# Experts' stage on the score banks, opened inside the last step of head 5

## What is computed

```python
xn = _layernorm(x)
qkv = einsum('bld,ed->ble', xn, w_qkv)      # 16 heads of 16, rope on q and k
attn = softmax(einsum('bhlm...', q, k) * scale)
s = einsum(attn, v) @ w_out.T
expert_idx = argmax(xn @ gate_w.T)          # 8 experts, one for each row
inter = square(relu(xn @ wg[e])) * (xn @ wu[e])
g = silu(inter @ wd[e])
return x + s * g
```

## Time and profile before

| | us |
|---|---|
| median of 3 runs (1563.64 to 1586.98) | 1569.34 |
| profiled execution | 1570.67 |
| its span | 1567.9 |
| TensorE busy (share of the span) | 1512.0 (96%) |
| DVE busy | 1383.9 (88%) |
| ACT busy | 1234.6 (79%) |
| mean share of full TensorE clock | 0.98 |

### The profile page before, as it was taken

One profiled execution on the slowest core, in us unless ns is written; L12 is line 12 of the kernel. 1 busy time (PEld: TensorE's weight loads), 2 busy tenths in 40 slices (PEclk: granted clock), 3 DMA queues, 4 the chain that ended last, 5 costly groups with the idle time before them and its releaser, 6 DMA issues.

```text
span 1567.9 us, 35612 instructions
## 1 busy us (share of the span) xinstructions
PE 1512.0 (96%) x13217; PEld 622.3 (40%) x13217; DVE 1383.9 (88%) x1497; ACT 1234.6 (79%) x2381; POOL 150.1 (10%) x206
## 2 busy tenths in 40 slices
PE   6997999999998999999999999999999999999997
PEld 4553333333374333333333333333333333333336
DVE  6678789999845999999999999999999999999706
ACT  4642388888756888888888888888888888888880
POOL 4432322100000222000010000000000000000100
PEclk9999599999999999999999999999999999999999
DMA  5873244326254445333333342233332433332203
GB/s 193 272 188 120 52 82 81 59 42 116 32 153 118 79 84 122 46 45 46 45 44 44 44 98 42 39 42 44 45 46 44 98 45 44 44 44 31 66 5 124
DMA packets 77909, 117.95 MB, mean 75 GB/s; under 512 B 29073, under 2 KB 64273, under 8 KB 70801
## 3 DMA queue, kind: packets, MB, share of 16 engines
q1 hardware_dynamic: 71808, 103.99, 33.9%
q0 software_dynamic: 3072, 8.39, 2.1%
q10 hardware_dynamic: 2896, 3.62, 0.6%
HBM read 75.31 MB, written 39.85 MB: 73 GB/s over the span
## 4 chain that ended last, share of the span: by engine, by line
PE 90%; ACT 3%; DVE 3%; DMA 2%; issue 2%; SPq 0%; ACTq 0%
PE ps L1139 42%; PE ps L1152 37%; PE ps L1071 3%; PE ps L1072 2%; DMA arena<-xs_d 1%; ACT arena L591 1%; ACT arena L555 1%; PE ps L1281 1%; DVE arena L699 1%; PE ps L1130 1%; PE ps L1095 1%; PE ps L1250 1%; PE ps L1238 1%; PE ps L1082 1%; DMA arena<-orec_d 1%
## 5 line engine op out<-in xcount | busy, mean ns | idle before, releaser
L591 ACT ACTIVATE arena<-ps 128x512 f32<-128x512 f32 x2048 | 1111.8, 595 | 179.0 <-PE ps L1139 91.1
L733 DVE TENSOR_REDUCE arena<-ps 128x1 f32<-128x1024 f32 x992 | 1205.5, 1221 | 38.8 <-PE ps L1130 32.9
L1139 PE MATMUL ps<-qs,ks 50*128 50x512 f32 x2048 | 759.0, 450 | 2.8 <-ACT arena L591 2.6
L1130 PE MATMUL ps<-ks,qs 48*128 48x512 f32 x1984 | 739.3, 453 | 4.5 <-DVE arena L733 2.9
L1152 PE MATMUL ps<-arena 128*32 128x256 f32 x8192 | 661.5, 395 | 7.4 <-ACT arena L555 7.0
L1139 PEld LDWEIGHTS ps<-qs,ks 50*128 50x128 f32 x2048 | 306.5, 187 | 434.1 <-issue 429.9
L1152 PEld LDWEIGHTS ps<-arena 128*32 128x32 f32 x8192 | 162.9, 108 | 386.2 <-issue 386.1
L1130 PEld LDWEIGHTS ps<-ks,qs 48*128 48x128 f32 x1984 | 298.6, 188 | 10.3 <-DVE arena L733 8.0
L1001 POOL COPY arena<-v_sb 128x256 f32 (+1 forms) x32 | 13.3, 416 | 953.2 <-ACT arena L555 938.1
L1071 PE MATMUL ps<-arena 128*128 128x512 f32 x128 | 67.8, 611 | 0.7 <-ACT arena L504 0.7
L513 ACT COPY arena<-ps 128x512 f32<-128x512 f32 x32 | 18.8, 586 | 54.8 <-PE ps L1072 54.8
(11 more groups left out here) (104 smaller groups left out, 510.4 us busy)
## 6 DMA issues: line engine op xcount, KB each, us to landing
qs<-parts_d SPq DMA_DIRECT2D x186, 128.0 KB, 4.5
ks<-parts_d SPq DMA_DIRECT2D x186, 128.0 KB, 5.1
parts_d<-arena SPq DMA_DIRECT2D x64, 256.0 KB, 2.6
xs_d<-arena SPq DMA_DIRECT2D x13, 384.0 KB, 3.5
arena<-xs_d SPq DMA_DIRECT2D x13, 384.0 KB, 3.9
ys_d<-arena SPq DMA_DIRECT2D x13, 384.0 KB, 2.8
onum_d<-arena SPq DMA_DIRECT2D x128, 32.0 KB
arena<-onum_d SPq DMA_DIRECT2D x3, 1024.0 KB
```

The costliest lines, as they stand in the source:

```text
L591: nc.scalar.activation(prob[kb % 2][:, c * W:(c + 1) * W], ps[:, bank, :], ACT.Exp, scale=SCALE).then_inc(exp_done[bank], 1)
L733: nc.vector.tensor_reduce(most[head_slot][:, tile, u:u + 1], ps[:, AB + 2 * u:AB + 2 + 2 * u, :], AX.XY, ALU.max).then_inc(a_reduced[u], 1)
L1130: ins = nc.tensor.matmul(ps[:, AB + c, :], qs[head_slot][ABASE:ABASE + KR, tile * P:(tile + 1) * P].bitcast(F32R), ks[head_slot][ABASE:ABA ...
L1139: nc.tensor.matmul(ps[:, bank, :], ks[s][0:KS, kb * P:(kb + 1) * P].bitcast(F32R), qs[s][0:KS, c * W:(c + 1) * W].bitcast(F32R), start=Tru ...
```

## The change

- The bank of a score comes from a table made for a pair. It counts 0, 1, 2 as before, but score 28 takes the second oldest bank instead of the oldest (`BENDS`), so that the last four scores of a pair have banks 2, 1, 0, 2.
- The experts' stage uses the score banks: transposes in bank 0, gate and up products in banks 1 and 2, and Y in banks 6 and 7 in turn (bank 7 alone before). A Y product waits for the Silu before the last one.
- `open_experts` issues, in the last step of head 5 between the two halves of the value product, the read of the first tile's expert and the first transposes. The step issues no scores of head 6. Three of them are issued in the stage's last iterations, the fourth behind the stage as before.
- The waits for the sums' copy and for DVE's last reduce move to the first transpose of hidden rows and the first Y.
- ACT takes a Silu of one element first, then copies the first turned tile, then the sums. The exponential of one column at the end is left out.
- SP asks for group `g + 3` where it asked for `g + 2`.
- `expert_of(i + 1)` stands at the end of iteration `i`; `expert_of(i)` stood before the product of tile `i`.

```diff
+    TB, EB, YB = 0, 1, 6
+        BENDS = (28,)
+        def banks_of_pair():
+            oldest_first, banks = list(range(NBB)), []
+            for n in range(2 * KB * QT):
+                banks.append(oldest_first.pop(1 if n in BENDS else 0))
+                oldest_first.append(banks[-1])
+            return banks
...
                 for g in range(NF // FG):
-                    if XR <= g + XR - 1 < NF // FG:
-                        load_sorted(g + XR - 1)
+                    if g + XR < NF // FG:
+                        load_sorted(g + XR)
                     store_sorted(g)
...
             def experts():
+                nc.scalar.activation(table_in[:, 1:2], table_in[:, 0:1], ACT.Silu)
+                turned_out(0)
                 sums_out(1, FB - 1)
-                turned_out(0)
...
-                act.wait_ge(xs_out, NF)
-                nc.scalar.activation(xsT[0][:, 0, 0:1], xsT[0][:, 0, 0:1], ACT.Exp)
...
-                        with_b = not (last_pair and s == 1 and kb == KB - 1)
+                        with_b = not (held_back or (last_pair and s == 1 and kb == KB - 1))
...
                             if c % 2:
                                 weigh_values(pi, s, kb, c // 2)
+                                if held_back and c == 1:
+                                    open_experts()
...
+            def open_experts():
+                for c in range(QT):
+                    pe.wait_ge(exp_done[b_bank(1, KB - 1, c)], past(b_before(FB - 1, 1, KB - 1, c) + 1))
+                pe.wait_ge(expert_ready, 1)
+                expert_of(0)
+                turn_sorted(0)
...
             def experts():
-                for u in range(2):
-                    pe.wait_ge(a_reduced[u], past(FB * 2 * KB + AHEAD - KB))
-                pe.wait_ge(o_out[1], past(FB))
-                turn_sorted(0)
...
+                    if i == NF:
+                        pe.wait_ge(loaded[0], (FB + 1) * (16 * LOADS))
+                        pe.wait_ge(shift_loaded[0], (FB + 1) * 64)
+                        pe.wait_ge(xs_out, NF)
+                        first_scores((0,))
                     if 1 <= i <= NF:
+                        if i == 1:
+                            pe.wait_ge(o_out[1], past(FB))
...
                     if i >= 2:
+                        if i == 2:
+                            pe.wait_ge(a_reduced[1], past(FB * 2 * KB + AHEAD - KB))
                         pe.wait_ge(inter_out, i - 1)
-                        if i >= 3:
-                            pe.wait_ge(y_out, i - 2)
-                        nc.tensor.matmul(ps[:, AB + 3, 0:D], interT[(i - 2) % 2], wd2[:, bass.ds(which.pop(i - 2), 1), :],
+                        if i >= 4:
+                            pe.wait_ge(y_out, i - 3)
+                        nc.tensor.matmul(ps[:, YB + i % 2, 0:D], interT[(i - 2) % 2], wd2[:, bass.ds(which.pop(i - 2), 1), :],
                                          start=True, stop=True).then_inc(y_done, 1)
-                pe.wait_ge(hu_ready, NF)
+                    if i + 1 < NF:
+                        expert_of(i + 1)
+                    if i == NF:
+                        pe.wait_ge(hu_ready, NF)
+                        first_scores((1, 2))
```

More of the change, by code:

```diff
@@ L279, in layer_kernel @@
         NP = NH // 2
-        BUSES = [[len(range((i - s) % NBB, KB * QT, NBB)) for i in range(NBB)] for s in range(2)]
-        PAIR_BUSES = [BUSES[0][i] + BUSES[1][i] for i in range(NBB)]
+        BENDS = (28,)
[5 more added lines that the diff above has]
+            return banks
+        BANKS = banks_of_pair()
+        PAIR_BUSES = [BANKS.count(i) for i in range(NBB)]
         NB2 = KB // 2
@@ L292, in past, with place_in_pair @@
             return n + 1
+        def place_in_pair(s, kb, c):
+            return (s * KB + kb) * QT + c
         def b_bank(s, kb, c):
-            return (kb * QT + c + s) % NBB
+            return BANKS[place_in_pair(s, kb, c)]
         def b_before(pi, s, kb, c):
-            bank = b_bank(s, kb, c)
-            return pi * PAIR_BUSES[bank] + (s * BUSES[0][bank] + (kb * QT + c) // NBB)
+            n = place_in_pair(s, kb, c)
+            return pi * PAIR_BUSES[BANKS[n]] + BANKS[:n].count(BANKS[n])
         block = ctx.enter_context(nc.Block())
@@ L574, in experts @@
                             act.wait_ge(inter_ready, i - 1)
-                        nc.scalar.activation(hr[i % 2], ps[:, AB + 1 + i % 2, 0:DE], ACT.Relu).then_inc(relu_done, 1)
+                        nc.scalar.activation(hr[i % 2], ps[:, EB + i % 2, 0:DE], ACT.Relu).then_inc(relu_done, 1)
                     if i >= 2:
@@ L580, in experts @@
                             act.wait_ge(y_stored[g % XR], g // XR * 16)
[L581 to L583 removed]
+                        nc.scalar.activation(ysb[g % XR][:, z, :], ps[:, YB + i % 2, 0:D], ACT.Silu).then_inc(y_out, 1)
             def exps(pi, s, first):
@@ L1191, in pair @@
                         for c in range(QT):
-                            if with_b and not (held_back and c == QT - 1):
+                            if with_b:
                                 score(b_pi, b_slot, (kb + 1) % KB, c)
@@ L1206, in turn_sorted, with expert_of, first_scores @@
                 for k in range(KC):
-                    last = nc.tensor.transpose(ps[:, AB, k * P:(k + 1) * P], xs[g % XR][:, z, k * P:(k + 1) * P], ident[:])
+                    last = nc.tensor.transpose(ps[:, TB, k * P:(k + 1) * P], xs[g % XR][:, z, k * P:(k + 1) * P], ident[:])
                 last.then_inc(xs_turned, 1)
+            which, packed = {}, {}
+            def expert_of(i):
+                g, z = divmod(i, FP)
+                if z == 0:
+                    packed[g] = pe.value_load(expert[0:1, g:g + 1], min_val=0, max_val=E ** FP - 1)
+                which[i] = pe.snap(packed[g] // E ** z % E, min_val=0, max_val=E - 1)
+            def open_experts():
[4 more added lines that the diff above has]
+                turn_sorted(0)
+            def first_scores(cs):
+                for c in cs:
+                    score(FB, 0, 0, c)
             def experts():
-                pe.wait_ge(expert_ready, 1)
                 pe.wait_ge(expert_weights, 16 * 6)
                 pe.wait_ge(pads_zeroed, 3)
-                for u in range(2):
-                    pe.wait_ge(a_reduced[u], past(FB * 2 * KB + AHEAD - KB))
-                pe.wait_ge(o_out[1], past(FB))
-                turn_sorted(0)
-                which, packed = {}, {}
-                def expert_of(i):
-                    g, z = divmod(i, FP)
-                    if z == 0:
-                        packed[g] = pe.value_load(expert[0:1, g:g + 1], min_val=0, max_val=E ** FP - 1)
-                    which[i] = pe.snap(packed[g] // E ** z % E, min_val=0, max_val=E - 1)
                 for i in range(NF + 2):
@@ L1231, in experts @@
                     if i < NF:
-                        expert_of(i)
                         pe.wait_ge(xs_out, i + 1)
```

6 lines of the change are left out of this document (3 added, 3 removed).

## The result

The changed kernel takes 1557.44 us (median of 20 runs, 1551.67 to 1578.59) against 1569.36 for the kernel before (20 runs). The ratio is 0.9932, 95% interval 0.9913 to 0.9951: 0.7% faster, some 10.7 us, which is within the 2%. The ratio leaves out runs that lie over 1.5% above the fastest of their kernel; the medians of all runs differ by 11.9. The forecast was 1555.5 with a range of 1548 to 1564. The time fell inside it, but the parts of the sum did not come out as they were forecast: in the profiles the experts' stage gave 4.7 less, the score banks 2.7 more.

What follows compares the result with a forecast made beforehand. The prediction took TensorE, busy 96% of a 1567.9 us span, as the bound. Opening 2.2, table 0.9, second to last Y 9.6, close 0.1 and banks 1.1 made 13.9 us, from 1569.34 to 1555.5, range 1548 to 1564.

Steps and rivals of the forecast that it cites:

- The rows' request: Experts' stage: asking for sorted rows one group earlier ends the transposes' stalls, about 5.2 us saved.
- The second Y bank: Experts' stage: two Y banks stop the 1.37 us loop from deciding; iteration becomes 1.25, about 4.4 us saved.
- the hidden one: Experts' stage: chain from gate/up product over Relu, DVE products and copy to hidden transpose; 2.40 us over two iterations.
- rival (a): Experts' stage: the hidden chain with ACT's queue holds the iteration at 1.37; the 4.4 is lost, 1560 us; chance 0.15.
- The register loads: Experts' stage: the load at every eighth tile, now behind Y, costs 0.4 us each, 1.6 in all for four.
- The opening: End of head 5: first transpose and register load inside the last step bring the first gate/up product 2.2 us earlier.
- The table: Start of the experts' stage: a dummy Silu puts the Silu table load into ACT's idle time, 0.9 us saved.
- The score banks: All heads: boundary waits behind odd heads save 2.8 us, late scores elsewhere lose 1.7, net 1.1.
- Rival (e): Score steps: the 0.04 us lateness at score 28 persists in each later step, 15 us lost, 1570; chance 0.03.
- (b): Experts' stage: the transfers of sorted rows become the bound, 1.4 us an iteration, 1559.5 us; chance 0.07.
- (d): Experts' stage: TensorE's clock falls in steady iterations that alternate banks; up to 43 us lost, 1599; chance 0.03.
- (c): TensorE at its floor of 1.21 us, loads hidden, head 6's slow restart missed: 6.5 us more gained, 1549; chance 0.10.

Runs made afterwards that it cites:

- late_rows: The changed kernel with SP asking for sorted rows one group later (g + 2), as before; second to last Y took 56.35 us, 4.25 more.
- one_y: The changed kernel with Y back in bank 7 alone; second to last Y 52.84 us in place of 52.10, ratio to the kernel before 0.9931.
- one_wait: The changed kernel without Y's own wait for the copy its hidden transpose had already waited for; second to last Y 50.50 us, 1.6 less.
- open_late: The changed kernel with the stage's opening behind head 5's last step instead of inside it; 40.02 us to the first gate/up product against 39.74.
- open_reduced: open_late with the waits for DVE's last two reduces back ahead of the first transposes; 41.85 us to the first gate/up product.
- copy_first: The changed kernel with DVE's copy of the turned hidden rows ahead of its two products; second to last Y 47.38 us, ratio to the kernel before 0.9874.
- two_bends: The changed kernel with a second bend at score 104 besides 28; heads 7 to 30 take 954.34 us.
- fill_exp: copy_first with five thrown-away TensorE products behind the last Y; 1550.94 us, ratio to the kernel before 0.9864, head 6 39.76 us.

## Why the prediction was right, and where it was not

**The rows' request: right.** The 5.2 for stalls measured 4.3 (late_rows); one group's lead was enough, and SP's queue held nothing up.

**The second Y bank: the loop was read rightly, what comes behind it was not.** The prediction took the loop of 1.37 apart from the earlier trace rows, and one_y gives 1.38. It then named the next chain, the hidden one, and put it at 2.40 for two iterations. It is 2.72. The first piece was exact: gate/up product to the end of the copy 1.58 forecast and 1.58 measured. The pieces behind it were priced short: 0.06 for the hand-over (measured 0.15), and from the earlier trace rows, where TensorE runs piece on piece, 0.11 from hidden transpose to Y (0.24) and 0.43 for Y (0.53). The earlier trace rows stand behind a stall on sorted rows, after which the hidden tile had long been ready; in the loop both products come straight behind the wait for the copy. Of the 0.32, one_wait shows 0.11 to be Y's own wait, needless but an instruction in the queue. The rest looks like TensorE's start behind a wait, which no run measured by itself. The mis-sized term is the iteration: 1.36 instead of 1.25, 37 x 0.11 = 4.1 of the 4.2 that second to last Y is short. The value lies outside the prediction's bound of 1.32 too, and it is rival (a) in mechanism: another loop of nearly the same length takes over. It had 0.15, on the argument that pieces follow each other without a wait. The prediction's own words, that the two chains are "level", should have weighed more: of two chains at 1.20 and 1.21, each waits for the other.

**The register loads: right.** 1.7 for the four in the count against 1.6.

**The opening: right in size, partly in reason.** 2.3 against 2.2. The prediction listed DVE's reduce as one of several things behind each other and gave the place inside the step the credit; open_late and open_reduced show that the wait for the reduce, with the register load that it leaves uncovered, is 1.9 of the 2.3 and the place 0.2, of which 0.04 is left by the second Y. It did foresee that the register load would push the step back. The gate/up product came 0.14 behind the start of the sums' copy.

**The table: 0.5 instead of 0.9.** First to second Y fell from 2.26 to 1.30, which is the 0.9 and a little more. But 0.4 was lost ahead of the first Y. Part of it is the sums' copy in ACT's queue, the thing that the prediction had only in its lower bound; 0.26 is DVE's copy behind its products, by copy_first, and the prediction had no term for that here. The load ends at 412.56 + 1.28 = 413.84 and the Silu starts at 413.85. For the further drain that the Trainium skill counts there (page "ScalarE: Activation LUTs", section "What ACT_TABLE_LOAD costs") the changed kernel's trace leaves no room, as that of before left none.

**The score banks: 3.8 instead of 1.1.** The sum had two halves. The gain of 0.20 at each odd head counted the late first score with it, which stays; what went is 0.17, 2.4 in all. The loss of 0.06 at 29 places, 1.7 in all, was taken from the 0.04 of the first late score in the earlier trace rows for all of them alike, though nothing in the trace of before said that it adds to the length of a head at score 28. There it does not; at the 14 boundaries it is 0.03 each (two_bends), 0.5 in all and already within the 2.4. The remaining 1.4 of the 3.8 is the shorter step, 2.460 for 2.467, that four of nine profiles with this table have; that part is not shown to be the table's. Rival (e), in which it persists, is out.

**Rivals.** (b): with copy_first the same transfers run at 1.21 per iteration, so they are no bound. (d): the clock stays at 1.00 through the whole stage, also at 1.21 an iteration with four banks in turn. Here the Trainium skill, page "TensorE: Matmul & The Clock Gate", section "A second HAM failure mode: psum-queue depth-cycling", warned of a loss; no trace of this case shows it. (c) needed the restart of head 6 to vanish, and nothing in the change does that; fill_exp shows what it takes.

**The total.** Minus 4.2 in the steady stage, minus 0.4 at the table, plus 2.7 at the banks, half of it the step's level; head 6's slow restart (1.0 more here) has no part in the code. That the median came within 2 us of the forecast is these errors cancelling, as far as it is not chance.

## What to carry to other kernels

Giving a second bank to the loop that holds an iteration is worth only the distance to the next chain. Write that chain out with every wait in it, price each piece behind a wait at what it takes behind a wait, and look on each engine for an operation whose input is ready early but that stands behind one that is late; with the second bank in place, moving one DVE copy was worth 4.7, more than six times what the bank had brought by itself. Before a gain is read from two profiles, cut both at the same instructions and set aside the stretches that the change does not touch. Where TensorE must rest before a long dense stretch, a few products that nobody reads can be worth more than the rest itself costs.

## What the runs showed of the hardware

**A fully busy TensorE can stay at half clock for a long time.** Behind the rest at the end of the stage late_rows ran 36.16 us at a granted clock of 0.50 (1.2 GHz) with TensorE busy for all of it, in the two windows above. In other profiles it was over after a few us in the same code. In head 0 it is the same. Windows of the changed kernel, then of open_late, with the same instructions:

```profile
172.00:185.00 13.00, 13.00 (x80) 4.19 (x72) 9.03 (x16) 6.55 (x13) 4.81 (x8) 0.50 0.04 11
185.00:200.00 15.00, 15.00 (x152) 5.48 (x144) 14.55 (x14) 12.68 (x24) 4.79 (x5) 0.99 0.13 45
```

```profile
185.00:200.00 15.00, 15.00 (x86) 4.77 (x86) 8.61 (x9) 7.60 (x14) 5.76 (x6) 0.50 0.13 45
200.00:217.00 17.00, 17.00 (x104) 5.69 (x108) 10.07 (x10) 8.98 (x17) 5.75 (x6) 0.56 0.15 54
```

Without the added products head 0 has 1 to 9 steps of 4.32 and one shorter one in place of 2.47, and takes 43.0 to 57.8. What decides how long it lasts is open; no code of these kernels goes with it. By an estimate it is most of the spread between runs of one kernel: among the runs of the changed kernel the mean granted clock is 0.983 in the shortest (1549.3 span) and 0.973 in one of 1566.1. A mean lower by 0.010 over 1560 us is 31 us at half clock in place of full, 16 us of lost work, and the spans differ by 16.8.

**A rest costs more than its length.** 2.5 us of rest behind the last Y made head 6 longer by 1.3 to 16. Five products of 256 columns in that rest took all of it away, in each of four profiles (39.7 or 39.8).

**A register load costs by where it stands.** In the changed kernel the load is 0.31 to 0.65 long with 0.15 of register arithmetic behind it. Issued while the value product still ran it is hidden (open_late), within a step it showed as 0.8 idle on the weight loads, and behind a wait that had emptied the queue the next product came 0.97 after the wait's end (open_reduced).

**A needless wait isn't free.** Leaving out one semaphore wait on TensorE's queue whose count had already been reached brought Y 0.11 nearer in every second iteration (one_wait).
